# Routing first, the shared expert between the experts, in the tail of a two-layer kernel

## The reference, cut to what matters

```python
logits = x @ gate_w.T                         # 64 experts
scores = softmax(logits); topk_w, topk_i = top_k(scores, 6)
# each expert takes at most 32 tokens, in the order of the tokens
g = buf @ w_gate[e]; u = buf @ w_up[e]        # 256 -> 176
y = (silu(g) * u) @ w_down[e]                 # 176 -> 256
out = sum over the chosen experts of weight * y
shared = (silu(x @ sw_gate) * (x @ sw_up)) @ sw_down   # 256 -> 352 -> 256, all tokens
x = layernorm(x + out + shared)
```

## Time and profile before

| | us |
|---|---|
| median of 3 runs | 1613.68 (1610.8 to 1615.94) |
| profiled execution | 1609.94 |
| its span, first to last instruction | 1608.2 |
| PE, DVE, ACT, POOL busy | 1452.3, 915.5, 576.8, 554.8 |

### The profile page before, as it was taken

The page is one execution under the profiler, slowest core; times in us unless marked ns, Lnnn a source line. Parts: engine busy times, 40 slices in busy tenths (PEclk is TensorE's granted clock), DMA queues, the critical chain, the costliest instruction groups (busy, mean ns, idle before and its releaser), DMA issues.

```text
span 1608.2 us, 23395 instructions
## 1 busy us (share of the span) xinstructions
PE 1452.3 (90%) x7898; PEld 1111.5 (69%) x7898; DVE 915.5 (57%) x2187; ACT 576.8 (36%) x1367; POOL 554.8 (35%) x483
## 2 busy tenths in 40 slices
PE   7899999999999999989999799999999998996660
PEld 6676767676767677666777588788788787774230
DVE  4576767676767677633342357566666656664013
ACT  4344444444444444622121133343334333331210
POOL 2754555454545455001012213512422412104122
PEclk9999999999999999999989899999999999898775
DMA  5000000000003000010000020110100006817954
GB/s 167 7 4 7 4 7 3 7 3 7 3 7 80 0 0 0 1 60 0 1 0 0 0 73 8 37 44 14 66 12 8 8 14 173 233 62 223 286 145 121
DMA packets 68090, 76.20 MB, mean 47 GB/s; under 512 B 14206, under 2 KB 55318, under 8 KB 68022
## 3 DMA queue, kind: packets, MB, share of 16 engines
q1 hardware_dynamic: 61533, 64.06, 13.8%
q0 software_dynamic: 3072, 4.72, 1.6%
q10 hardware_dynamic: 3416, 6.52, 1.4%
HBM read 66.22 MB, written 9.08 MB: 47 GB/s over the span
## 4 chain that ended last, share of the span: by engine, by line
PE 76%; DVE 8%; DMA 7%; POOL 4%; issue 3%; ACT 2%; POOLq 0%; DVEq 0%; ACTq 0%
PE ps L1533 37%; PE ps L1620 9%; PE ps L1642 9%; PE ps L1627 6%; DMA sums_dram<-y_out,sidx 6%; PE ps L1672 4%; PE ps L1762 4%; PE ps L1968 1%; DVE acc L1116 1%; PE ps L1839 1%; PE ps L1829 1%; PE ps L1644 1%; POOL wq L553 1%; POOL qk L612 1%; POOL wo L553 1%
## 5 line engine op out<-in xcount | busy, mean ns | idle before, releaser
L1070 DVE TENSOR_REDUCE mx<-ps 128x1 f32<-128x128 f32 (+3 forms) x256 | 125.7, 491 | 156.6 <-PE ps L1644 151.6
L612 POOL TENSOR_TENSOR qk<-q,ksb 128x512 f32<-128x512 f32 x64 | 82.6, 1291 | 303.2 <-ACT q L845 212.6
L1642 PE MATMUL ps<-kT,qT 128*128 128x128 f32 (+3 forms) x512 | 174.8, 450 | 3.2 <-ACT probs L761 3.2
L761 ACT ACTIVATE probs<-ps,nm 128x128 f32<-128x128 f32 (+3 forms) x256 | 134.8, 527 | 114.8 <-DVE nm L1073 107.1
L1014 DVE TENSOR_TENSOR prod<-ps,rope_sb 128x1024 f32<-128x1024 f32 x128 | 150.8, 1220 | 19.5 <-PE ps L1533 14.0
L1620 PE MATMUL ps<-pT,c_tok 128*128 128x512 f32 (+3 forms) x512 | 155.1, 446 | 0.7 <-ACT pT L704 0.7
L704 ACT ACTIVATE pT<-ps 128x256 f32<-128x256 f32 (+3 forms) x256 | 93.5, 441 | 154.0 <-PE ps L1672 154.0
L495 POOL TENSOR_TENSOR qT<-prod 64x512 f32<-64x512 f32 x64 | 81.6, 1275 | 179.9 <-PE ps L1644 93.9
L1620 PEld LDWEIGHTS ps<-pT,c_tok 128*128 128x128 f32 x512 | 92.0, 189 | 67.2 <-issue 30.6
L1627 PE MATMUL ps<-U,oT 128*128 (+1 forms) x512 | 124.6, 386 | 0.7 <-ACT oT L704 0.7
L495 POOL TENSOR_TENSOR kT<-prod 64x512 f32<-64x512 f32 x64 | 81.6, 1274 | 121.6 <-DVE prod L1014 113.9
(11 more groups left out here) (238 smaller groups left out, 2645.4 us busy)
## 6 DMA issues: line engine op xcount, KB each, us to landing
eg<-in_L_ffn_w_gate_dram SPq DMA_DIRECT2D x16, 704.0 KB
eg<-in_L_ffn_w_up_dram SPq DMA_DIRECT2D x16, 704.0 KB
ed<-in_L_ffn_w_down_dram ACTq DMA_DIRECT2D x9, 640.0 KB
ed<-in_L_ffn_w_down_dram SPq DMA_DIRECT2D x7, 640.0 KB
ksb<-ks_dram SPq DMA_DIRECT2D x16, 256.0 KB, 3.3
rows_dram<-rows SPq DMA_DIRECT2D x4, 640.0 KB, 3.8
acc<-in_L_attn_x_dram SPq DMA_DIRECT2D x4, 512.0 KB
wq_in<-in_L_attn_wq_dram SPq DMA_DIRECT2D x8, 256.0 KB, 2.8
```

The source lines that it names most:

```text
L612: nc.gpsimd.tensor_tensor(qk[:], q3[:], ksb[b % 2][:], ALU.mult).then_inc(qk_ready, 1)
L761: nc.scalar.activation(probs[hh][:, off:off + (i + 1) * P], ps[:, BS + i % 2, 0:(i + 1) * P], ACT.Exp, bias=nm[:, hh, i:i + 1], scale=SCAL ...
L1070: nc.vector.tensor_reduce(mx[:, hh, i:i + 1], ps[:, BS + i % 2, 0:(i + 1) * P], AX_X, ALU.max).then_inc(max_ready, 1)
L1642: pe.matmul(ps[:, bank, 0:(i + 1) * P], qT[:, hh, b, i * P:(i + 1) * P], kT[:, hh, b, 0:(i + 1) * P], start=True, stop=False)
```

## The change

It changes six things:

- The statistics of the third norm go into the last chunk of the attention, for batches 0 to 2 (`statistics16`, in `chunk3`, with `root16` on GpSimd); those of batch 3 stand behind the last accumulation.
- Routing goes ahead: rows, logits, choice and lists of the four batches are laced with the shared products of batches 0 and 1. There are three x3T buffers instead of two. `rows4(2)` waits for the stores of batch 0, `rows4(3)` for those of batch 1.
- `store_rows` stores each batch twice, with scores to `rows_dram` and without to `sums_dram` (batch 0 a third time, 128 rows behind the table). The base is now the rows alone; `store_base` is gone.
- The shared products use one pair of banks (5 and 6) and one `gated4`. ScalarE copies their result into `acc` (`shared_rows`). The first product of batch 2 stands between the transposed indices; the other two and the three of batch 3, with the down products of both batches, stand behind groups 1, 3, 5, 7, 9, 11 and 13.
- A group has one bank for each step in place of two, and the sum is copied into `xg[:, s, 0:D]`, the room of the gathered rows, so no copy waits for a scatter. The scatters still wait for one another.
- The ring has six buffers in place of seven. At the end `fin` is loaded and the shared part `acc` is added to it before the statistics.

```diff
-        EXPERTS_AT = (169, 188, 104, 131, 150, 80, 20)
+        fin = place("fin", 40, [P, TILES, D])
+        EXPERTS_AT = (169, 188, 104, 131, 150, 85)
@@ SyncE
             def store_rows(b):
                 sp.wait_ge(scored, b + 1)
-                wait_past(sp, rows_stored, 16 * b)
-                sp.dma_start(rows_dram[b * T:(b + 1) * T, :].rearrange("(i p) n -> p i n", p=P), rows[b % 2][:]).then_inc(rows_stored, 16)
+                if b:
+                    sp.wait_ge(rows_stored, 32 * b + 16)
+                here = rows[b % 2]
+                sp.dma_start(rows_dram[b * T:(b + 1) * T, :].rearrange("(i p) n -> p i n", p=P), here[:]).then_inc(rows_stored, 16)
+                sp.dma_start(sums_dram[b * T:(b + 1) * T, :].rearrange("(i p) n -> p i n", p=P), here[:, :, 0:D]).then_inc(rows_stored, 16)
+                if b == 0:
+                    sp.dma_start(sums_dram[TOK:TOK + P, :], here[:, 0, 0:D]).then_inc(rows_stored, 16)
@@ VectorE, last chunk
+                        if last and b and i == 2:
+
+                            dve.wait_ge(added3, 4 * n)
+                            statistics16(b - 1, acc)
@@ VectorE, rows4
                 if b >= 2:
 
-                    dve.wait_ge(rows_stored, 16 * (b - 1))
+                    dve.wait_ge(rows_stored, 32 * (b - 1) + 16)
@@ VectorE, the tail
             rows4(0)
             add3(BLOCKS * TPB - 1, TILES - 1)
+            dve.wait_ge(added3, BLOCKS * TPB)
+            statistics16(BATCH - 1, acc)
             x3_rests(0)
             dve.wait_ge(sw_hi, 1)
             rest(gwT[1][:], ps[:, 2, 0:KD * E1].rearrange("p (k e) -> p k e", k=KD), gwT[0][:]).then_inc(sw_lo, 1)
+            rows4(1)
+            top_logits(0)
             dve.wait_ge(sw_hi, 2)
             rest(sw[1][:], sw_in[:], sw[0][:]).then_inc(sw_lo, 1)
-            for b in range(BATCH):
-                route4(b, b == BATCH - 1)
+            choose(0)
+            x3_rests(1)
+            list_tokens(0)
+            top_logits(1)
+            rows4(2)
+            choose(1)
+            x3_rests(2)
+            hidden4(0, 0)
+            hidden4(0, 1)
+            list_tokens(1)
+            hidden4(0, 2)
+            top_logits(2)
+            rows4(3)
+            choose(2)
+            x3_rests(3)
+            list_tokens(2)
+            hidden4(1, 0)
+            top_logits(3)
+            choose(3)
+            hidden4(1, 1)
+            list_tokens(3)
+            merge_lists()
+            hidden4(1, 2)
+            take_slots()
@@ TensorE, gate_up4: one pair of banks
-                wait_past(pe, hid4_ready, b * FT1 + max(m - 1, 0))
+                wait_past(pe, hid4_ready, b * FT1 + m)
@@ TensorE, the tail
             logits(0)
+            turn_x3(1)
+            turn_marked(0)
+            logits(1)
+            turn_x3(2)
             pe.wait_ge(sw_lo, 2)
-            for b in range(BATCH):
-                route4(b, b == BATCH - 1)
+            gate_up4(0, 0)
+            gate_up4(0, 1)
+            turn_marked(1)
+            gate_up4(0, 2)
+            logits(2)
+            turn_x3(3)
+            down4_products(0)
+            gate_up4(1, 0)
+            turn_marked(2)
+            logits(3)
+            gate_up4(1, 1)
+            turn_marked(3)
+            gate_up4(1, 2)
+            down4_products(1)
+            turn_slots()
@@ TensorE, the experts
             for s in range(GROUPS):
                 turn_hidden(s)
+                if s + 1 < GROUPS:
+                    gate_up(s + 1)
                 if s + 2 < GROUPS:
                     rows_of(s + 2)
-                if s + 1 < GROUPS:
-                    gate_up(s + 1)
                 down(s)
                 if s:
                     sum_repeats(s - 1)
+                if s in (1, 3):
+                    gate_up4(2, (s + 1) // 2)
+                if s == 5:
+                    down4_products(2)
+                if s in (7, 9, 11):
+                    gate_up4(3, (s - 7) // 2)
+                if s == 13:
+                    down4_products(3)
@@ VectorE, the sum and the end
             def summed_rows(s):
                 dve.wait_ge(y_summed, s + 1)
-                if s >= 3:
-
-                    dve.wait_ge(scattered, 16 * (s - 2))
-                nc.vector.tensor_copy(y_out[s % 3][:], ps[:, 6 + s % 2, 0:D]).then_inc(y_copied, 1)
+                nc.vector.tensor_copy(xg[:, s, 0:D], ps[:, 4, 0:D]).then_inc(y_copied, 1)
             def last_statistics(b):
                 dve.wait_ge(sums_loaded[b], sums_loaded_first[b] + 16)
+                dve.wait_ge(shared_done, 2 * b + 2)
+                at = slice(b * TPB, b * TPB + TPB)
+                link(nc.vector.tensor_tensor(fin[:, at, :], fin[:, at, :], acc[:, at, :], ALU.add))
                 settle()
+                statistics16(b, fin)
```

More of the change, by code:

```diff
@@ L181, in program @@
         gwT = [place(f"gwT{h}", 31 + 0.5 * h, [P, KD, E1], F32R) for h in range(2)]
-        x3T = [[place(f"x3T{i}{h}", 32 + 18 * i + 4 * h, [P, KD, T], F32R) for h in range(2)] for i in range(2)]
-        gated4 = [place(f"gated4{h}", 58 + 2 * h, [M1, T]) for h in range(2)]
-        hid4 = place("hid4", 62, [M1, FT1, T])
-        rows = [place(f"rows{i}", 40 + 5 * i, [P, TPB, ROW]) for i in range(2)]
-        e4 = place("e4", 68, [P, TPB, E1])
-        marked = place("marked", 69, [P, 2, 2, E1])
@@ L218, in program @@
-        meanvar5 = place("meanvar5", 129.5, [P, TILES, 2])
-        vareps5 = place("vareps5", 129.75, [P, TILES])
-        rstd5 = place("rstd5", 129.875, [P, TILES])
-        EXPERTS_AT = (169, 188, 104, 131, 150, 80, 20)
+        x3T = [[place(f"x3T{i}{h}", 32 + 8 * i + 4 * h, [P, KD, T], F32R) for h in range(2)] for i in range(3)]
+        rows = [place(f"rows{i}", 56 + 5 * i, [P, TPB, ROW]) for i in range(2)]
+        e4 = place("e4", 66, [P, TPB, E1])
+        marked = place("marked", 67, [P, 2, 2, E1])
@@ new lines, in program @@
+        lists = place("lists", 68, [P, BATCH * CAP])
+        nmx4 = place("nmx4", 68.5, [P, TPB])
+        sm4 = place("sm4", 68.5625, [P, TPB])
+        top4 = place("top4", 68.625, [P, TPB, 8])
+        cand = [place(f"cand{i}", 69 + i, [P, 2 * P]) for i in range(2)]
+        merged = [place(f"merged{i}", 66 + i, [E1, 2 * BATCH * CAP]) for i in range(2)]
+        countdown = place("countdown", 71, [P, BATCH, 2 * P])
+        kept = place("kept", 75, [E1, CAP])
+        lanes = place("lanes", 75.25, [E1, 4, GROUPS])
@@ new lines, in program @@
+        gated4 = place("gated4", 76, [M1, T])
+        hid4 = place("hid4", 78, [M1, FT1, T])
+        stat16 = place("stat16", 16.5, [P, TILES, 6])
+        meanvar16 = place("meanvar16", 16.875, [P, TILES, 2])
+        vareps16 = place("vareps16", 17.0625, [P, TILES])
+        rstd16 = place("rstd16", 17.125, [P, TILES])
+        xg = place("xg", 56, [P, GROUPS, ROW])
+        same = place("same", 40, [P, GROUPS, P])
+        masked = place("masked", 18, [P, 2, P])
+        wtmp = place("wtmp", 19.25, [P, GROUPS, 4])
@@ new lines, in program @@
+        tri = place("tri", 19.5, [P, P])
+        y_in = [place("y_in0", 31, [P, D]), place("y_in1", 84, [P, D])]
+        xsT = [place(f"xsT{h}", 126 + h, [P, KD, P]) for h in range(2)]
+        actE = place("actE", 128, [P, I1])
+        hE = place("hE", 128.75, [P, I1])
+        hET = place("hET", 129.5, [IH, 2, P])
+        quarter = place("quarter", 130.5, [P, 4])
+        lane = place("lane", 130.53125, [P, 1])
+        wslot = place("wslot", 130.5625, [P, GROUPS])
+        idxf = place("idxf", 130.625, [P, GROUPS])
@@ L621, in chunk3 @@
                             centre_wv3(c + 1)
+                        if b and i == 3 and last:
+                            root16(b - 1, 8 + b)
                     if b == 1 and not last:
@@ L962, in gate @@
                 wait_past(act, hE_ready, s)
-                nc.scalar.activation(actE[:], ps[:, 1 + s % 2, 0:I1], ACT.Silu).then_inc(actE_ready, 1)
+                nc.scalar.activation(actE[:], ps[:, 1, 0:I1], ACT.Silu).then_inc(actE_ready, 1)
             def outputs4(s):
```

300 lines of the change are left out of this document (132 added, 168 removed).

## The result

The changed kernel takes 1628.1 us (median of four, 1625.2 to 1630.2) where the kernel before took 1614.6 on the same chip: ratio 1.0087, interval 1.0066 to 1.0109. It is slower by 0.9%; the forecast was 1625.2 us and slower. The profiled execution has a span of 1623.4 us, 15.2 more than before.

The account below looks back on a forecast made before the run. The prediction took 16 accumulating scatters, one after the other, then the VectorE-bound last norm, as the bound. Gather +2.1, scatters +4.3 and last norm +5.1 gave +11.5 us on 1613.7: 1625.2 us, 0.7% slower, range 1612 to 1636.

Parts of the forecast that it names:

- Part 1: Ahead of routing: statistics moved into the attention's last chunk cost +2.4 us (0 to 6.6); first logits start at 1377.6.
- the other two terms: First logits: 1.4 us earlier without waiting for statistics and power, 2.3 later because batch 3's statistics stand in between.
- Part 2: In routing, VectorE waits for stores queued on SyncE behind expert weights: idle 14 us, from about 1391 to 1405.1.
- The 2.5 us for the added bytes: In the store wait: three transfers carry 1.3 MB instead of 0.65 MB, the added 0.65 MB at some 260 GB/s.
- the rival that shortens the wait: In routing, stores land as on an empty queue, 9.4 us earlier: 1615.8 us, the same within 0.3%; chance 0.12.
- Part 3: From batch 2's rows to the first gather: engine queues followed put the gather at 1461.7, +2.1 us.
- Part 4: First gather to last scatter: the smaller ring makes the full DMA stretch 8 us longer, costing the scatters +4.3 us.
- The seven products: Shared products between experts, 25 us at the high clock, cost nothing: PE needs some 4 of 8 us per group.
- Part 5: In the last norm: four VectorE additions of the shared part, one per batch, cost +5.1 us (4.9 to 5.6).
- The rule on the shared port pair: In the last norm: VectorE additions and GpSimd's power exclude each other; up to 3.3 us more if additions always came second.
- the expert loop becomes the bound: In the expert loop, at the low clock a group with products takes 10.2 us in place of 8: 1632; chance 0.12.
- TensorE's own work bounds the routing: Ahead of the gather, PE's own work stays the bound, so the gather comes 24 us earlier: 1598.8 us; chance 0.08.

Follow-up runs that it names:

- again: The changed kernel once more, unedited, profiled on another chip beside the kernel before: 1621.0 us, ratio 1.0081 (1.0051 to 1.0112).
- first group: again, stores_pool, ring6 and no_add, run on one chip beside the kernel before, whose median there was 1609.0 us.
- stores_pool: The changed kernel with the stores of the rows issued from GpSimd's queue in place of SyncE's: 1613.9 us, ratio 1.0022 to the kernel before.
- ring6: The kernel before with six expert buffers in place of seven and nothing else: 1612.7 us, ratio 1.0028 (1.0014 to 1.0042).
- no_add: The changed kernel without the four additions of the shared expert's part in the last norm: 1617.2 us, ratio 1.0061 to the kernel before.
- no_seven: The changed kernel without the seven shared products between the experts and ScalarE's and VectorE's work for them: 1621.6 us, ratio 1.0060 to the kernel before.
- second and third group: Later sets of kernels, each set on one chip beside the kernel before, whose medians there were 1613.0 and 1613.8 us.

## Why the prediction was right, step by step

The side, the size (1625.2 against 1628.1, inside the range) and the mechanism named for it came out. The sum of +11.5 stands against +15.2 in the first profile, +8.7 in the profile of again, and +13.5 in the medians. Against the profile without the long step the forecast is 2.8 too high; the long step, which it doesn't have, makes up for that. If the kernel before has no such step on those chips, the agreement of the medians is partly luck. On the first group's chip, where no profile has it, the medians differ by 11.9 us.

- **What bounds the kernel before.** Right: the 16 scatters, one after the other, then VectorE. In the changed kernel TensorE's products end with them up to the twelfth scatter. A change that took 19 us of TensorE's work out of the routing stretch moved the first gather by +1.2 to +2.0.
- **Part 1, too high.** The first logits were at 1373.08, 1.2 us earlier than in the earlier trace rows. But all of the changed kernel's program was 2.2 us ahead by then, seen at the additions that answer (925.4 against 927.6). In again, 1.2 us behind at that point, they were at 1376.6. Both give +1.0 to +1.1 where the forecast had +3.3. If the other two terms are right (-1.4 and +2.3), the statistics in the chunk cost next to nothing, where +2.4 was taken; no run shows it by itself. What came instead: these logits took 5.30 us at the low clock (0.50). The 3.66 of the earlier trace rows, which was taken for that, was not all at the low clock: it was 0.76 in the mean in 1374 to 1378.
- **Part 2, right.** VectorE was there at 1389.25 (1401.72 - 12.47), forecast 1391; the stores landed at 1401.6, forecast 1405.1; 12.5 us of idle time against 14. The 2.5 us for the added bytes was too much: from the first issue to the last landing are 13.4 us (1388.24 to 1401.62), where one transfer had taken 12.6. stores_pool shows the cause, the place in SyncE's queue, with a correction: SyncE was 6.8 us late with the first store because it was busy issuing (scores complete at 1381.4, issue at 1388.24), and the last two transfers then took 9.2 and 10.2 us, much as they do from GpSimd (10.1 and 10.0). What was said of the rival that shortens the wait is right in its price too: 1615.8 stood there, a ratio of 1.0013, and stores_pool has 1.0022.
- **Part 3, right.** From the end of the rows of batch 2 to the gather 55.2 us were followed out. In again it was 55.0 (1406.65 to 1461.62), in the other two 57.7. The order by hand is what carries this number. Behind the wait the granted clock was 0.50 until 1405 and 1.00 from 1410 on, so the first product ran at the low clock for the most part and the next ones did not, as the forecast had it. Why 19 us less work on TensorE brought nothing is there as well: lists, products on one pair of banks, and rows wait for each other in turn.
- **Part 4, right in the mechanism, too high by a third.** ring6 gives +3.0 and again +3.5 from the first scatter to the last landing, for +4.3. The term that was mis-sized is the price of a scatter in the additional stretch: 9.7 us a step was taken, and the rows of ring6 have 8.4 and 7.7 (1534.16 to 1542.52 to 1550.24); 8 x (1 - 4.5/8) is 3.5. The seven products were hidden, as said. In the executions with the long step the scatters take only 1.4 us more; they start 9 us later, so fewer of them can meet full DMA engines.
- **Part 5, right.** Five us, of which no_add takes 4.3 away. The rule on the shared port pair (the Trainium skill, SBUF — State Buffer, Who interferes with whom) would have added up to 3.3 here. The addition that was running when a power of GpSimd's began wasn't slowed; GpSimd's was:

```profile
1605.01 1.22 DVE L1552 TENSOR_TENSOR fin<-fin,acc 128x1024 f32<-128x1024 f32 x1
...
1605.19 1.96 POOL L597 TENSOR_TENSOR rstd<-vareps,halfp 128x4 f32<-128x4 f32 x1 [9.51 <-DVE vareps L1291]
1608.38 1.24 POOL L597 TENSOR_TENSOR rstd<-vareps,halfp 128x4 f32<-128x4 f32 x1 [1.24 <-DVE vareps L1291]
```

  The power that started 0.2 us after the addition took 1.96 us. The same power took 1.04 us in no_add, which has no addition; if it had waited here until the addition ended at 1606.23, it would have taken 2.08. The later ones took 1.24, and the additions behind them began only 0.1 us before their ends and took 1.22 as ever. That the two exclude each other fits this one meeting; that an addition comes second to a power that has long to run, on which the +3.3 hung, does not happen here.
- **The rivals.** That the expert loop becomes the bound (1632) did not come: TensorE's clock rose to 0.92, the reason given against it, and in no_seven the loop was no shorter. It was near, as the twelfth scatter shows. That TensorE's own work bounds the routing (1598.8) did not come either: it stood still for 14.4 us at one place and for some 12 us more in pieces behind it.
- **Not foreseen: the step from gather to first scatter.** It was taken as unchanged. It is 1.9 us shorter in the profile of again and 7.5 and 7.2 longer in the others, with the cause open.

## What to carry to other kernels

Work that is taken off the busiest engine is worth only what the next wait in line leaves of it: before moving products, look where every instruction that now waits stands in its stream, and what is to be issued in front of the transfer that it waits for (12.5 us of idle time with the stores behind the weights on SyncE, 4.4 with the same stores issued from GpSimd). Look on from there: a gather that comes earlier is nothing if the same work stands between it and its user. Work put beside a stretch that waits for DMA can be free, and part of its own time comes back, since TensorE kept a higher clock with it here (0.92 against 0.69).

## What the runs showed of the hardware

- TensorE's granted clock was 0.50 (1.2 GHz of 2.4) from 1373 on, for 13.1 us of work in 29 us, through the 14.4 us pause and until 1405; it was 0.60 in 1405 to 1410 and 1.00 in 1410 to 1420. In the expert loop it was 0.92 in the mean of 50 us with the shared products and 0.69 without them. A group's first products took 2.57 us at the lower level and 1.32 at the higher.
- In nine profiles (the first of the changed kernel and all of the second and third group) answers of TensorE reached ScalarE later than the modelled end of the product, in the first one 4.5 us later and SyncE in the same instant. They fell into the stretch in which GpSimd's gathers were issued and landed. The other profiles (before and the first group) have the same gathers and no such answer. The cause wasn't found.
- Issuing took time on the queue's engine when the DMA engines were full: one pair of down weights held SyncE for 5.96 us, and a store of 128 rows for 3.6 (other stores 0.4 to 0.5 us after 1404). Stores issued from GpSimd in the same stretch took it 0.6 to 1.0 us each and landed within 1 us of the same time after the start of their issue.
